# Head attention on one core: the order of TensorE's value units and output products in even turns

## The reference

```python
qkv = x @ w_qkv + b_qkv
qkv = qkv.reshape(Bq, Lq, NUM_HEADS, 3 * HEAD_DIM)      # 16 heads of 64
q, k, v = jnp.split(qkv, 3, axis=-1)
k = k + pos_enc[None, :, None, :]
attn = jnp.einsum('blhd,blgd->blhg', q, k) / scale
attn = jax.nn.softmax(attn, axis=-1)
out = jnp.einsum('blhg,blgd->blhd', attn, v)
out = out.reshape(Bq, Lq, NUM_HEADS * HEAD_DIM)
return out @ w_out + b_out
```

## Time and profile before

| what | value |
|---|---|
| median of 3 runs | 1058.34 us (1057.93 to 1058.45) |
| the profiled execution's own time | 1057.54 us |
| its span in the trace | 1055.8 us |
| time outside the span | 1.74 us |
| head attention, first to last turn | about 20 to 189 us of the span |

### The profile page before, as it was taken

The page is one execution under the profiler, slowest core; times in us unless marked ns, Lnnn a source line. Parts: engine busy times, 40 slices in busy tenths (PEclk is TensorE's granted clock), DMA queues, the critical chain, the costliest instruction groups (busy, mean ns, idle before and its releaser), DMA issues.

```text
span 1055.8 us, 22183 instructions
## 1 busy us (share of the span) xinstructions
PE 1039.9 (98%) x8784; PEld 664.3 (63%) x8784; DVE 787.9 (75%) x1239; ACT 563.9 (53%) x912; POOL 784.2 (74%) x514
## 2 busy tenths in 40 slices
PE   9999999999999999999999999999999999999998
PEld 7898898777645545545545545545545545477886
DVE  4658767477777888878878878878878888675554
ACT  5644444555565555555555555555555555544442
POOL 5778998745458898899999999999999999800000
PEclk9999999999999999999999999999999999999999
DMA  7323233543100300000000000000000000000000
GB/s 243 133 82 100 85 122 119 155 139 120 40 1 1 111 1 2 1 1 2 1 1 1 2 1 1 2 1 2 1 2 1 1 1 1 2 0 11 11 1 21
DMA packets 32679, 40.23 MB, mean 38 GB/s; under 512 B 4544, under 2 KB 24384, under 8 KB 31296
## 3 DMA queue, kind: packets, MB, share of 16 engines
q1 hardware_dynamic: 32256, 38.80, 11.4%
q10 hardware_dynamic: 320, 0.01, 0.0%
HBM read 28.97 MB, written 9.70 MB: 37 GB/s over the span
## 4 chain that ended last, share of the span: by engine, by line
PE 80%; DVE 8%; POOL 3%; issue 3%; ACT 3%; DMA 1%; SPq 1%; DVEq 0%; POOLq 0%; ACTq 0%
PE o_ps L1720 18%; PE mx_ps L1673 7%; PE st_ps L1692 5%; PE st_ps L1698 5%; PE st_ps L1695 5%; PE ha_banks L641 5%; PE bank L2149 4%; PE bank L2151 3%; PE bank L2150 3%; PE mx_ps L1610 3%; PE pj_ps L1625 3%; PE mx_ps L1605 3%; PE ha_banks L694 2%; PE ha_banks L705 2%; DVE mx_part L1925 2%
## 5 line engine op out<-in xcount | busy, mean ns | idle before, releaser
L2063 POOL TENSOR_TENSOR acc<-acc,prob 128x1024 f32<-128x1024 f32 x188 | 456.5, 2428 | 34.2 <-POOL acc L2063 23.7
L1863 ACT ACTIVATE prob<-st_ps 128x1024 f32<-128x1024 f32 x256 | 248.3, 1022 | 209.1 <-PE st_ps L1698 106.7
L1720 PE MATMUL o_ps<-prob,v_cur 128*64 128x512 f32 x1024 | 243.4, 596 | 0.0
L1925 DVE TENSOR_REDUCE mx_part<-mx_ps 128x1 f32<-128x512 f32 x258 | 168.0, 678 | 22.4 <-PE mx_ps L1673 13.5
L1720 PEld LDWEIGHTS o_ps<-prob,v_cur 128*64 128x64 f32 x1024 | 69.1, 137 | 120.9 <-issue 80.7
L1928 DVE TENSOR_REDUCE mx_part<-mx_ps 128x2 f32<-128x1024 f32 x78 | 95.6, 1225 | 49.7 <-PE mx_ps L1673 49.7
L1673 PE MATMUL mx_ps<-k_hi,q_hi 64*128 64x512 f32 x414 | 112.1, 457 | 2.5 <-DVE mx_part L1928 0.5
L1698 PE MATMUL st_ps<-q_hi,d_lo 64*128 64x512 f32 x512 | 101.7, 391 | 0.0
L1673 PEld LDWEIGHTS mx_ps<-k_hi,q_hi 64*128 64x128 f32 x414 | 46.9, 183 | 84.8 <-issue 51.1
L2063 POOL TENSOR_TENSOR acc<-prob 128x1024 f32<-128x1024 f32 x32 | 76.6, 2393 | 23.6 <-ACT prob L1863 23.6
L949 POOL TENSOR_TENSOR ha_wide<-ha_pt,ha_own 128x512 f32<-128x512 f32 x64 | 74.4, 1186 | 9.4 <-ACT ha_pt L905 9.2
(11 more groups left out here) (393 smaller groups left out, 2157.5 us busy)
## 6 DMA issues: line engine op xcount, KB each, us to landing
w_tile<-w_rows SPq DMA_DIRECT2D x72, 128.0 KB, 2.9
v_rows<-ha_v SPq DMA_DIRECT2D x8, 1024.0 KB, 4.1
ha_vt<-v_rows SPq DMA_DIRECT2D x16, 512.0 KB, 4.2
q_max<-mx_turned SPq DMA_DIRECT2D x128, 1.0 KB
h_w<-in_h SPq DMA_DIRECT2D x2, 1024.0 KB, 8.3
w_raw<-in_w SPq DMA_DIRECT2D x8, 192.0 KB, 4.0
head_wkv<-in_wkv SPq DMA_DIRECT2D x2, 512.0 KB, 4.7
m_w<-in_m SPq DMA_DIRECT2D x3, 256.0 KB, 3.0
```

What stands on the lines that cost most here:

```text
L1720: mm = pe.matmul(o_ps[rows(h), :], v_cur[:, m % 2, j, rows(h)], prob[:, (16 * m + slot) % RING, h, :], start=(j == 0), stop=(j == KT - 1), ...
L1863: act.activation(prob[:, n % RING, :, :], st_ps[:, slot % 2, :, :], ACT.Exp, scale=SCALE).then_inc(s_exp, 1)
L1925: dve.reduce_max(mx_part[:, h, i, keys:keys + 1], maxima_banks(q, n)[h], AX_X).then_inc(s_mxr, 1)
L2063: pool.tensor_tensor(total, old, new, ALU.add).then_inc(s_acc, 2)
```

## The change

In even turns V8 and V9 no longer stand between the scores and the output products. The first half of the output products comes directly behind the scores, then V8, V9, V10 and V11 in a row, then the second half, then Q0 and Q1 as before. Odd turns keep their order, and so does turn 0, which has no output products; so seven turns change, 2, 4, 6, 8, 10, 12 and 14. No instruction is added or removed, and no other engine's queue is touched.

```diff
@@ -724,12 +724,14 @@
         tensor_scores(pe, i, 1)
 
 
-        for b, u in units(i, range(ahead, 2)):
-            tensor_project(pe, b, u)
+        early = range(ahead, 2)
+        if i % 2:
+            for b, u in units(i, early):
+                tensor_project(pe, b, u)
         for quarter in range(4):
             if i >= 2:
                 tensor_out(pe, i - 2, quarter // 2, quarter % 2)
-            for b, u in units(i, (2 + quarter,) if i % 2 else ((), (2, 3), (), (4, 5))[quarter]):
+            for b, u in units(i, (2 + quarter,) if i % 2 else ((), (*early, 2, 3), (), (4, 5))[quarter]):
                 tensor_project(pe, b, u)
         if i >= 1:
             tensor_turn(pe, i - 1)
```

## The result

| | before | after |
|---|---|---|
| median | 1058.34 us (1057.93 to 1058.45) | 1063.98 us (1063.73 to 1065.79) |
| profiled execution's span | 1055.8 us | 1061.9 us |

The change makes the kernel 5.6 us slower by the medians, 0.53%; 1063.9 us was forecast. The ratio, which is taken over all runs and not between the medians, is 1.0061, with a 95% interval of 1.0043 to 1.0079.

A forecast was written before the change was run, and what follows sets the result against it. TensorE, busy 98% of the span, was taken as the bound, with a chain through VectorE, GpSimd and ScalarE reaching K4. Seven pairs summed to 5.6 us over 1058.34, giving 1063.9 us; range 1060.8 to 1066.4.

The forecast's parts named there:

- TensorE's own part: TensorE's queue in even turns: the new order and the lost cover delay it by 7 x 0.16 + 0.53 = 1.65 us.
- The bank wait and restart: V10 on TensorE waits 0.24 us for V8's bank, then pays a first unit's 0.80 again; +0.16 a turn.
- The lost cover: First half of products, no longer behind V8 and V9, waits for `wide[0]`: 0.11 us in turn 8, 0.53 together.
- The chain behind V8 and V9: Late V8 and V9 delay VectorE's sum, GpSimd's probabilities and ScalarE's exponentials before K4: +1.07 us plus first-half lateness.
- The slack: Lateness odd turns absorb before K4: 0.52 us in turns 3 and 13, 0.06 in 9, zero in 7 and 11.
- It adds up: GpSimd falls back into step at every even turn, so each pair of turns pays anew; together 5.6 us.
- The rival that the delay is paid once: After the first late pair TensorE stays behind and GpSimd's lateness costs nothing new: 1061.1 us, chance 6%.
- V11 does not wait: On TensorE, V9 frees its bank 2.43 us after V8's start; V11 wants to start at 2.54, margin 0.11.
- the double wait: V10 and V11 both wait 0.36 us in the row: 1 to 3 us more, 1066, chance 9%.
- The weights of V10: V10's weights load with its matmul after waiting; loading them ahead would save 0.10 a turn, 0.7 us in all.
- The clock: Rival: short TensorE gaps lower the clock; at half clock seven turns cost up to 72 us: 1130, chance 1%.
- The gain of 0.18 a turn from one switch fewer: TensorE's even-turn stretch would take 4.08 us instead of 4.26 if the bank cost nothing.

The follow-up runs named there:

- The changed kernel with the sum first: Changed kernel, with VectorE computing the sum and its reciprocal ahead of V8 and V9 in even turns: 1059.68 us.
- Two repairs at two links of it: Changed kernel with VectorE's sum ahead of V8 and V9, 1059.68 us; changed kernel with one key bias ahead of GpSimd's probabilities, 1060.90 us.
- two extra reductions in seven turns: Kernel before, with two unused reductions on VectorE between the reads of V8 and V9 and the sum in even turns: 1064.32 us.

## Why the prediction held, step by step

- **TensorE's own part** was right in kind and too small in size. The bank wait and restart were put at 0.16 a turn; in turns 4, 12 and 14, where no cover is lost, the stretch from the scores' end to the second half grew by 0.21, 0.23 and 0.27. The missing 0.06 is the read of V8: VectorE begins it 1.07 after the unit's start (110.17 to 111.24), not 1.00. The prediction took this term from the wrong unit. Its 1.00 is V10's (109.11 to 110.11), while the same rows have 1.08 for V8 (106.43 to 107.51), and in turns 2 to 14 of all kernels here V8 keeps 1.06 to 1.09 wherever VectorE is not busy past it. Why the two units differ stays open.
- **The lost cover** was put at 0.11 in turn 8 and measured 0.15, as TensorE goes on 0.10 behind the end of `wide[0]` (106.68 + 2.30 to 109.08), not 0.06. Over turns 2 to 14 the stretch grew by 0.56, 0.21, 0.37, 0.38, 0.36, 0.23 and 0.27: the own part is 2.4 us where 1.65 was forecast. The changed kernel with the sum first has 2.25 of it left, less the K4 waits that the same edit takes away.
- **The chain behind V8 and V9** was right: 4.60 behind the scores' end, 4.54 forecast for turn 8 (4.43 + 0.11). Two of its terms were off and cancel by luck: the 0.07 and the 0.04 above are in it, and the sum follows the read of V8 by 1.23 (111.24 to 112.47) where 1.31 was forecast. Two repairs at two links of it, on VectorE and on GpSimd, each take away the waits at K4, and the delay alone, with TensorE in its old order, makes the loss.
- **The slack** of 0.52, 0.06 and zero was right: the pairs come out within 0.1 us each. Where it is 0.52, the larger own part eats into what was forecast for K4: its waits in turns 3 and 13 are 0.23 and 0.21, below the 0.4 to 1.2 of the prediction, with the pairs as forecast.
- **It adds up.** GpSimd waits for TensorE's turned probabilities at the start of turn 8 in the changed kernel as before (0.98 us idle, the first GpSimd row of turn 8), and two extra reductions in seven turns cost 6.5 us, not 1.2. The rival that the delay is paid once is out.
- **V11 does not wait**, as forecast with 0.11 of margin; of the double wait nothing is seen.
- **The weights of V10** load with its matmul after the wait, in all seven turns, and the restart costs 0.79 (111.99 to 112.78) where 0.80 was forecast. The Trainium skill ("TensorE: Matmul & The Clock Gate", "Step-by-step: what each phase is for") says that weight loads are pulled ahead of running matmuls. The trace agrees for V9 (0.23 ahead) and not for V10, which waits for its bank, nor for V8, the first behind another kind of matmul (0.01 ahead each).
- **The clock** stayed at 1.00, in turns 8 and 9 as in each turn from 2 to 14.

The forecast of the sum was off by 0.2 us (5.62 and 5.85), much less than the 0.7 by which TensorE's own part was: where the chain rules, only what delays V8 counts, and the longer row behind it does not. That the medians meet within 0.1 us (1063.9 and 1063.98) is luck beyond that, as the kernel before alone has medians from 1057.66 to 1058.34 over the three groups. The gain of 0.18 a turn from one switch fewer, which is all that the order could have brought, was never seen, as the row spends it at V10's bank.

## What to carry to other kernels

When an operation is moved on the busiest engine, follow its result and not only its engine: what is read late holds up everything queued behind that read, related or not. Here a sum that has nothing to do with the values stood behind their reads, and three queues on it stopped TensorE in the next turn. The cheap test for such a case is to delay the suspected instruction alone in the old kernel, and the cheap repair is to take what does not depend on the late result ahead of it in that queue.

## What the runs showed that had not been expected

- The same program part ahead of turn 2 took between 37.64 and 38.63 us from the span's start over the profiled runs, with no edit in it for turns 0 and 1 of TensorE. Differences of spans below a microsecond should be read from the starts of turns, not from whole spans.
- Taking the row of four apart did not shorten turns 2, 6, 8 and 10, since the second half of the products then arrived ahead of `wide[1]`. In turn 8 the wait taken away and the one that showed behind it are of one size (0.16 and 0.17 us).
